# A fused two-layer kernel on one core: high products of the first expert tile ahead, block 0's matrices fetched by two queues, gate table loaded first

## What is computed

```python
w = weights[subjects]                                    # 8 matrices 64x64, one chosen per sample
y = einsum('bct,bcd->bdt', x, w)                         # "mix"
gate, up = split(y @ ternary(w_gate_up).T)               # 2048 each; weights quantized in groups of 64
h = silu(gate) * up
x = x + rms_norm(h) @ ternary(w_proj).T                  # layer 0
H = x @ W.T + scal * ((x @ A[idx].T) @ Bm[idx].T)        # one of 8 rank 16 adapters per sample
logits = (H @ router_w.T + router_b).reshape(T, 512, 8)  # 8 logits per token AND output column
c = weights of the top 2 of softmax(logits), renormalized, scattered over the 8 experts
    # c[t, e] sums over the 512 columns
x = x + sum_e c[t, e] * (H @ expert_w[e].T + expert_b[e])   # layer 1
```

## Time and profile before

| | |
|---|---|
| median of 3 runs | 2350.64 us (2349.07 to 2351.0) |
| the profiled execution | 2351.97 us |
| its span | 2350.2 us, 30421 instructions |
| granted TensorE clock, mean | 0.995 |
| VectorE busy | 1669.3 us, 71% |
| ScalarE busy | 1148.8 us, 49% |
| GpSimd busy | 8.9 us |
| moved by DMA | 184.61 MB, mean 79 GB/s |

### The profile page before, as it was taken

One profiled execution on the slowest core, in us unless ns is written; L12 is line 12 of the kernel. 1 busy time (PEld: TensorE's weight loads), 2 busy tenths in 40 slices (PEclk: granted clock), 3 DMA queues, 4 the chain that ended last, 5 costly groups with the idle time before them and its releaser, 6 DMA issues.

```text
span 2350.2 us, 30421 instructions
## 1 busy us (share of the span) xinstructions
PE 2301.7 (98%) x10280; PEld 1897.4 (81%) x10288; DVE 1669.3 (71%) x2497; ACT 1148.8 (49%) x1685; POOL 8.9 (0%) x16
## 2 busy tenths in 40 slices
PE   6999999999999999999999999998899999999999
PEld 5777888888888887888888888887688888888887
DVE  7985434334343435888888888999988888888883
ACT  6764333323332324788888888887322222222221
POOL 0000000000000000000000000000000000000000
PEclk9999999999999999999999999999999999999999
DMA  5314202111111115211111111215322222222220
GB/s 197 105 44 137 74 19 74 43 54 51 54 54 37 71 36 201 75 65 62 62 54 66 58 58 63 67 62 182 142 91 87 94 78 78 94 80 76 94 80 22
DMA packets 106589, 184.61 MB, mean 79 GB/s; under 512 B 12466, under 2 KB 45746, under 8 KB 105266
## 3 DMA queue, kind: packets, MB, share of 16 engines
q1 hardware_dynamic: 54946, 124.84, 15.2%
q10 hardware_dynamic: 51600, 59.25, 7.6%
HBM read 122.72 MB, written 61.34 MB: 78 GB/s over the span
## 4 chain that ended last, share of the span: by engine, by line
PE 90%; issue 5%; DVE 3%; ACT 1%; DMA 1%; ACTq 0%; SPq 0%; POOL 0%; POOLq 0%; DVEq 0%
PE slot L1445 17%; PE plane L1576 10%; PE plane L1578 10%; PE plane L1580 10%; PE ex L1618 10%; PE ex L1620 10%; PE ex L1622 10%; PE pj L1458 8%; PE slot L1498 3%; PE slot L1420 1%; PE slot L1487 1%; PE slot L1477 1%; PE slot L1430 0%; DMA eraw<-in_ewT 0%; DMA eb_sb<-in_eb 0%
## 5 line engine op out<-in xcount | busy, mean ns | idle before, releaser
L1618 PE MATMUL ex<-ew_hi,hb 128*128 128x512 f32 x1024 | 400.8, 391 | 16.6 <-DVE ew_lo L1332 11.3
L1445 PE MATMUL slot<-y_hi,wgu 128*128 128x512 f32 x1024 | 403.1, 394 | 2.3 <-DVE q_scale L1002 1.2
L1576 PE MATMUL plane<-rw_hi,hb 128*128 128x512 f32 x1024 | 399.5, 390 | 1.6 <-ACT plane L834 0.9
L1620 PE MATMUL ex<-ew_hi,hb 128*128 128x512 f32 x1024 | 400.4, 391 | 0.0
L1622 PE MATMUL ex<-ew_lo,hb 128*128 128x512 f32 x1024 | 400.3, 391 | 0.0
L1578 PE MATMUL plane<-rw_hi,hb 128*128 128x512 f32 x1024 | 399.2, 390 | 0.0
L1445 PE MATMUL slot<-y_lo,wgu 128*128 128x512 f32 x1024 | 399.1, 390 | 0.0
L1580 PE MATMUL plane<-rw_lo,hb 128*128 128x512 f32 x1024 | 399.1, 390 | 0.0
L942 ACT ACTIVATE ex<-eb_sb 128x512 f32<-128x512 f32 x248 | 149.3, 602 | 460.0 <-DVE acc L1371 395.8
L1304 DVE SCALAR_TENSOR_TENSOR lead_in<-code_in,wts 128x1024 bf16<-128x1024 bf16 x256 | 311.5, 1217 | 1.8 <-DVE code_in L1249 0.4
L1618 PEld LDWEIGHTS ex<-ew_hi,hb 128*128 128x128 f32 x1024 | 193.4, 189 | 58.5 <-issue 7.9
(11 more groups left out here) (128 smaller groups left out, 3148.3 us busy)
## 6 DMA issues: line engine op xcount, KB each, us to landing
hb<-h_scratch SPq DMA_DIRECT2D x34, 512.0 KB, 3.3
h_scratch<-ht ACTq DMA_DIRECT2D x64, 256.0 KB, 3.0
code_scratch<-half_code SPq DMA_DIRECT2D x64, 256.0 KB, 2.0
half_in<-code_scratch SPq DMA_DIRECT2D x32, 512.0 KB, 3.3
hb<-h_scratch ACTq DMA_DIRECT2D x30, 512.0 KB, 3.6
q_raw<-in_w_ffn SPq DMA_DIRECT2D x21, 512.0 KB, 3.4
x_scratch<-x_res ACTq DMA_DIRECT2D x8, 1024.0 KB, 4.4
rraw<-in_rwT SPq DMA_DIRECT2D x8, 1024.0 KB, 11.0
```

The source lines that it names most:

```text
L1445: last = mm(slot[s % 2][:, g, :], wgu[:, c, r * P:(r + 1) * P], y[:, c, :], start=(c == 0 and v == 0), stop=(c == DC - 1 and v == 1))
L1576: mm(plane[b][:, :, :], hb[:, u, c, 0, :], rw_hi[:, w, c, o], start=False, stop=False, skip_group_check=True)
L1618: mm(ex[e][:, :], hb[:, u, c, 0, :], ew_hi[:, e, c, :], start=(first and c == 0), stop=False, skip_group_check=True)
L1620: mm(ex[e][:, :], hb[:, u, c, 1, :], ew_hi[:, e, c, :], start=False, stop=False, skip_group_check=True)
```

## The change

1. Block 0's eight gathers are shared: SyncE fetches samples 0 to 3 (`mixw_in`), GpSimd samples 4 to 7 (`mixw0_in`), ahead of its constants. TensorE waits for both.
2. SyncE's next loads change order: x_res and three gathers for block 1, then raw tiles 3 and 4, then the other five gathers.
3. ScalarE runs a Silu of one column as its first activation, and the first `square` waits for it.
4. Expert weights lie in DRAM as one run of 8 KB for each expert and partition (before: four of 2 KB), loaded without the spill of tile NT-2 between them.
5. `eb_sb` lies in the memory of `bias_sb` and is loaded once the last plane is seeded, ahead of that spill; `xin` is loaded after the last half's tournament, behind the spill and the loads of tile 2's lead and codes.
6. TensorE does the 64 products with `ew_hi` of tile 0 for all experts, then the 32 with `ew_lo`.
7. ScalarE makes the six splits 2 to 7 ahead of the last two `stand`. VectorE does the last half without its join, splits 3 to 7, the eight expert steps of tile 0, the two joins, the eight bias steps, and decode and totals of tile 2 by themselves; then tiles 1 and on as before.
8. ScalarE's first pair of tiles is written out: the seeds after tile 0 come ahead of the weighing of tile 2, and the store of tile 0 waits for the bias steps.

```diff
+        eb_sb = sb("eb_sb", [P, E, D], F32, p4)
+        p4.close()
         bias_sb = sb("bias_sb", [P, 2, E, HO], F32, p2)
...
-            gather_mix(0, mixw, mixw_in)
+            gather_mix(0, mixw, mixw_in, range(SPB // 2))
...
+            sp.dma_start(x_res[:, :, :], one(XB, 1)).then_inc(xmix1_in, 16)
+            gather_mix(1, mixw1, mixw1_in, range(3))
             load_raw(3)
             load_raw(4)
-            sp.dma_start(x_res[:, :, :], one(XB, 1)).then_inc(xmix1_in, 16)
-            gather_mix(1, mixw1, mixw1_in)
+            gather_mix(1, mixw1, mixw1_in, range(3, SPB))
...
-                    sp.dma_start(eraw[:, e, :, :], EWT[e]).then_inc(eraw_in[e], 16)
-                if b == 0:
-                    spill(NT - 2, 0, 2 * NT - 3, 2 * NT - 2, 2 * NT - 2)
+                    sp.dma_start(eraw[:, e, :, :].rearrange("p c o -> p (c o)"), ewT[e]).then_inc(eraw_in[e], 16)
             load_h(1, 1)
-            sp.wait_ge(joined, 2 * NT)
-            sp.dma_start(xin[:, 0, :], X1T[0]).then_inc(x1_in[0], 16)
+            sp.wait_ge(seeded, NT * PT)
             sp.dma_start(eb_sb[:, :, :], eb).then_inc(eb_in, 16)
-            sp.dma_start(xin[:, 1, :], X1T[1]).then_inc(x1_in[1], 16)
+            spill(NT - 2, 0, 2 * NT - 3, 2 * NT - 2, 2 * NT - 2)
             load_lead(2, 0)
             sp.wait_ge(decoded, 2)
             load_halves(2)
+            sp.wait_ge(lead_ready, 2 * NT)
+            sp.dma_start(xin[:, 0, :], X1T[0]).then_inc(x1_in[0], 16)
+            sp.dma_start(xin[:, 1, :], X1T[1]).then_inc(x1_in[1], 16)
             spill(NT - 1, 1, 2 * NT - 1, 2 * NT, 2 * NT)
...
         def _(pool):
+            pool.wait_ge(dconst, 1)
+            pool.wait_ge(subject_in, 16)
+            for q in range(SPB // 2, SPB):
+                v = pool.value_load(subject_i[0:1, q:q + 1], min_val=0, max_val=E - 1)
+                r = (q % 2) * C
+                pool.dma_start(mixw[r:r + C, q // 2, r:r + C], cond_w[bass.ds(v * C, C), :]).then_inc(mixw0_in, 16)
+
...
+            act.wait_ge(dconst, 3)
+            nc.scalar.activation(sq[:, 0:1], ones_col[:, :], ACT.Silu).then_inc(table_in, 1)
             quant_in(0)
...
-            split_expert(2)
+            for e in range(2, E):
+                split_expert(e)
             stand(NT - 1, 0)
-            split_expert(3)
-            split_expert(4)
             stand(NT - 1, 1)
-            for e in range(5, E):
-                split_expert(e)
...
             def store(n, u):
+                if isinstance(n, int) and n == 0:
+                    act.wait_ge(bias_step, E)
...
-                    weigh(m * 2 + (u + 2), u, m + 1)
+                    if not (isinstance(m, int) and u == 0):
+                        weigh(m * 2 + (u + 2), u, m + 1)
                     for e in range(E):
                         seed_expert(m * 2 + u, e)
+                    if isinstance(m, int) and u == 0:
+                        weigh(2, 0, 1)
...
             for e in range(3):
                 split_expert(e)
-            half(NT - 1, 1, 1, NT // 2 - 1)
-            split_expert(3)
-            split_expert(4)
-            join(NT - 1, 1)
-            for e in range(5, E):
+            half(NT - 1, 1, 1, NT // 2 - 1, joins=False)
+            for e in range(3, E):
                 split_expert(e)
...
+            def bias(e):
+
+                if e:
+                    dve.wait_ge(bias_step, e)
+                nc.vector.scalar_tensor_tensor((res if e == E - 1 else acc)[:, 0, :], eb_sb[:, e, :], c_ring[:, 0, e:e + 1],
+                                               acc[:, 0, :], ALU.mult, ALU.add).then_inc(bias_step, 1)
...
+            for e in range(E):
+                expert(0, e, 0, 0)
+            for s in range(2):
+                join(NT - 1, s)
             dve.wait_ge(eb_in, 16)
+            dve.wait_ge(exp_step, E)
             for e in range(E):
-                bias(0, e, 0, 1)
-            for n in range(4):
+                bias(e)
+            decode(2, 2)
+            for e in range(E):
+                total(2, e, 2)
+            for n in range(1, 4):
                 tile(n, n, n // 2)
...
-            experts(0, 0, first=True)
+            def first_experts():
+
+                pe.wait_ge(hb_in[0], NT // 2 * 16 + 16)
+                for e in range(E):
+                    if e >= 4:
+                        pe.wait_ge(evac, NT * PT - 3 + e - 4)
+                    pe.wait_ge(ehi, e + 1)
+                    for c in range(DC):
+                        for v in range(2):
+                            mm(ex[e][:, :], hb[:, 0, c, v, :], ew_hi[:, e, c, :], start=(c == 0 and v == 0), stop=False)
+                for e in range(E):
+                    pe.wait_ge(elo, e + 1)
+                    for c in range(DC):
+                        last = mm(ex[e][:, :], hb[:, 0, c, 0, :], ew_lo[:, e, c, :], start=False, stop=(c == DC - 1))
+                    last.then_inc(ex_filled, 1)
+
+            first_experts()
             experts(0, 1)
...
-        "ewT": g["L1_ffn_expert_w"].transpose(2, 0, 1).reshape(D, E * D),
+        "ewT": g["L1_ffn_expert_w"].reshape(E, D, DC, P).transpose(0, 3, 2, 1).reshape(E, P, DC * D),
```

More of the change, by code:

```diff
@@ L304, in build @@
         mixw_in = sem("mixw_in")
+        mixw0_in = sem("mixw0_in")
         xres_in = sem("xres_in")
@@ L412, in _, with gather_mix @@
         def _(sp):
-            def gather_mix(i, w, done):
-                for q in range(SPB):
+            def gather_mix(i, w, done, samples=range(SPB)):
+                for q in samples:
                     v = sp.value_load(subject_i[0:1, bass.ds(i * SPB + q, 1)], min_val=0, max_val=E - 1)
@@ L558, in _ @@
             load_halves(2)
+            sp.wait_ge(lead_ready, 2 * NT)
+            sp.dma_start(xin[:, 0, :], X1T[0]).then_inc(x1_in[0], 16)
+            sp.dma_start(xin[:, 1, :], X1T[1]).then_inc(x1_in[1], 16)
             spill(NT - 1, 1, 2 * NT - 1, 2 * NT, 2 * NT)
             def ahead(n, u, wait):
-                if isinstance(n, int) and n == 0:
-                    sp.wait_ge(bias_step, 1)
-                else:
-                    sp.wait_ge(exp_step, wait)
+                sp.wait_ge(exp_step, wait)
                 sp.dma_start(xin[:, u, :], one(X1T, n + 2)).then_inc(x1_in[u], 16)
@@ L686, in square @@
             def square(i, j, h):
-                if not (first_block(i) and j == 0):
+                if first_block(i) and j == 0:
+                    act.wait_ge(table_in, 1)
+                else:
                     act.wait_ge(ss_ready, i * HC + j)
@@ L1366, in expert @@
                     dve.wait_ge(summed, n * E + E)
-                    base = xin
                 dve.wait_ge(ex_filled, n * E + (e + 1))
@@ L1370, in expert @@
                     dve.wait_ge(out_done[u], trip * 16)
-                nc.vector.scalar_tensor_tensor((res if e == E - 1 else acc)[:, u, :], ex[e][:, :], c_ring[:, k, e:e + 1],
-                                               base[:, u, :], ALU.mult, ALU.add).then_inc(exp_step, 1)
+                nc.vector.scalar_tensor_tensor((res if e == E - 1 and not first else acc)[:, u, :], ex[e][:, :],
+                                               c_ring[:, k, e:e + 1], (xin if e == 0 else acc)[:, u, :],
+                                               ALU.mult, ALU.add).then_inc(exp_step, 1)
             def tile(n, k, pair):
```

43 lines of the change are left out of this document (15 added, 28 removed).

## The result

The median is **2340.11 us** (2339.09 to 2341.39, 6 runs) against 2350.82 for the kernel before in the same session (2349.07 to 2352.15, 6 runs): ratio 0.9955, 95% interval 0.9945 to 0.9965. The forecast was 2340.1. The profiled execution took 2339.39 us, its span is 2337.7, the granted clock 0.997.

The account below looks back on a forecast made before the run. TensorE was taken as the bound, busy 2301.7 of 2350.2 us. Gains of 2.7, 1.0 and 6.8 sum to 10.5; from the profiled 2351.97 that gives 2341.5, and 1.3 lower for the median, 2340.1; 8-in-10 range 2338.6 to 2345.6.

Parts of the forecast that it names:

- Gathers, -2.7: Start of block 0: sharing the eight gathers between SyncE and GpSimd lets the mix start at 11.3, saving 2.7 us.
- a margin of 2.4: Start of block 0: gathers landed by 8.9, while the mix needs them at 11.3.
- one of the signs of being wrong: Start of block 0: a wait of the mix for a transfer beyond 11.3 would show the prediction wrong.
- The rival of late gathers: Start of block 0: GpSimd's gathers land late, giving 2345.3 us, or 2342.7 in a middle case; chance 0.20.
- Table, -1.0: Before the first gate product: the early one-column Silu removes the later table load for which VectorE waited, saving 1.0 us.
- SyncE's order, 0: Start: SyncE's reordered loads delay nothing, raw tile 3 arriving with 2.4 us to spare; 0 us.
- Transition, the chain: First expert tiles: VectorE's work in its new order, from first split at 1629.32 to tile 1's first expert step at 1683.2.
- Transition, TensorE: First expert tiles: tile 2's e=1 begins at 1689.8 against 1696.58, saving 6.8 us.
- 2 to 6 us: First expert tiles: a new TensorE idle of this length stands before tile 2.
- lower clock beyond e=1: Transition rival: the lower clock outlasts the start of tile 2's e=1, costing 1.7 us; whole short-transition rival's chance 0.12.
- The sum: Whole kernel: gathers 2.7, table 1.0 and transition 6.8 add to a gain of 10.5 us.

Follow-up runs that it names:

- the experiment: All eight gathers of block 0 on SyncE again, with SyncE's loads in their old order, against the changed kernel: 2345.21 us, ratio 0.9973.
- the repeated pair: The changed kernel and the kernel before, each run once more unchanged: 2340.05 and 2350.29 us, one run each.

## Why the prediction was right, point by point

- **Gathers, -2.7: measured -2.4** (13.98 to 11.56; 2.3 by the experiment). SyncE's fourth goes out at 7.07 (computed 6.8), GpSimd's at 7.19. The step that was mis-sized is the landing: I took 2.1 us from the issue, so 8.9 on either queue, and a margin of 2.4. It took 4.4 us on SyncE's queue and 4.1 on GpSimd's, and the mix waited 0.18 us for SyncE's, until 11.56. That is one of the signs of being wrong that the prediction named. The 2.1 us were those of the eighth gather of the kernel before, issued when little else was in flight. The windows show it, first of the kernel before at that gather, then of the changed kernel at the fourth (us, busy of PE, PEld, DVE, ACT, POOL, granted clock, DMA share, GB/s):

```profile
11.90:14.00 2.10, 0.02 (x1) 0.05 (x1) 2.00 (x3) 0.36 (x1) 0.00 (x0) 1.00 0.26 55
```

```profile
7.00:11.50 4.50, 1.04 (x2) 0.13 (x2) 4.27 (x7) 2.11 (x3) 1.23 (x5) 1.00 1.05 361
```

At 361 GB/s all 16 DMA engines are busy, with raw tiles 1 and 2 and with x_res, which the change itself puts right behind the fourth gather. In the kernel before the fourth gather was in some 3.6 us after its issue. How much of the difference is x_res, no run here tells. In the kernel with the bias steps first the issues run 1.0 us later and the landing only 0.35 later, so the landing hardly follows the issue there. An error of 2.6 us in the landing cost 0.2, because TensorE's second mean keeps it until 11.38 in any case; that part of the hit is luck. The margin was all gone: in other executions of the same start the mix waits up to 0.79 (at 11.91, again with the bias steps first). The rival of late gathers named the wrong queue: both land late, and GpSimd's ahead of SyncE's. The Trainium skill ("DMA: Bandwidth & Descriptors", section "Issuing engines are not separate DMA queues") would have had the issue time "usually small"; here halving it was worth the 2.3 us. Its rule in "SBUF — State Buffer", section "SBUF: two separate sides", that GpSimd's DMAs starve beside a two-port operation of VectorE, does not show in these rows: the pitch of the issues stays 1.15 us, and GpSimd's gathers land no later than SyncE's beside them.
- **Table, -1.0: measured -0.97**, the whole of VectorE's idle (1.06 by the interval from TensorE's first gate and up product). Together with the mix's own length (5.52 for 5.70) the start gives 2.42 + 0.18 + 0.97 = 3.6 of the 3.66 seen at the first gate product. It passes on undiminished: `bias_sb` is loaded 3.77 earlier.
- **SyncE's order, 0**: raw tiles 3 and 4 go at 11.99 (computed 12.4), and no engine waits for them.
- **Transition, the chain.** Computed 53.9 from the first split (1629.32 to 1683.2), measured 53.48. By parts, computed and measured: three splits 6.6, 6.61; half 8.7, 8.86; five splits 11.1, 11.01; expert steps 6.3, 6.17; joins 1.4, 1.20; bias steps 6.3, 6.17; decode 3.4, 3.43; totals 10.1, 10.03. The totals do stand at 1.25 each without a partner. Tile 1's first expert step comes at 1676.93, not near 1679.5 as foreseen: 2.1 of that is the clock in the third column and no work of the change. xin was issued at 1639.04 and is not waited for, nor is the third expert's weight.
- **Transition, TensorE.** From the router's last product to tile 2's e=1 I computed 62.4 (1689.8 - 1627.38); it is 62.15, against 69.20 before: -7.05. The wait before tile 2, "2 to 6 us", is 4.80. That mark hides 0.4: tile 2's e=1 still begins at the lower clock until 1684.2, so the stretch to the end gains only 6.6 (722.82 - 716.20). The rival's "lower clock beyond e=1" came true at a quarter of its price. **-6.8 predicted, -6.6 measured** in this pair of executions, -5.7 in the repeated pair and -6.4 by the means.
- **The sum** had 10.5; the rows of the first pair give 10.3, the means over all executions 9.9 and the medians 10.7. That the forecast met the median of 2340.11 to the tenth is luck: a stretch of lower clock moves one execution by two, and the same interval differs by up to 0.9 between two executions of one kernel. What held is the mechanism of each term and its size to about half a microsecond.
- **What was not foreseen** is the idle of 3.6 us in the high products, 1.91 of it for the eighth expert's weights, whose load ends at 1637.5. The prediction had the weights in by 1641 in the old time, which is 1635.1 here, so 2.4 late; the bias table and other loads are issued from 1622.77 on, beside them. It cost nothing, since the low parts end later in any case.

## What to carry to other kernels

When the bound engine waits at a transition, write the feeding engine's work there as a chain with its prices, and ask of each link whether the next consumer needs it now: here eight totals and a decode for the tile after next stood in front of tile 1's first step, and moving them behind it won another 6.7 us (2340.11 to 2333.38). A reordering that is worth nothing alone may be worth something on top of another (here the high products: 0 alone, 2.1 us beside VectorE's new order), so test them alone and together. The time of a transfer from issue to landing holds only for the traffic in which it was read: 2.0 us for a gather at 55 GB/s were 4.4 at 361. And where single stretches of lower clock move a whole run by 2 us, compare kernels by intervals between marks, over more than one execution, before a median is believed.

## What the runs showed of the hardware that was not expected

- TensorE's granted clock falls in stretches whose length differs between executions of one kernel. The same work between two marks takes 178.6 us in seven of the fourteen traces and 180.7 to 180.9 in the other seven, nothing between; the clock falls there at a wait of 4.10 us that all fourteen have.
- At the start likewise. Of the five executions of the new start in which the mix begins by 11.69, none has the products at 20 us at the lower clock, and the first gate product comes at 24.17 to 25.16; of the four in which it begins between 11.82 and 12.23, three have (26.53 to 27.11; one of these is the kernel with the table load). So a late landing of the gathers may cost more than its wait of 0.2 us in some runs; four cases don't prove it, and the kernels with all gathers on one queue have the lower clock at the same place too (mix at 13.83 and 15.69), while the kernel before (13.98) does not.
- A DMA issued by GpSimd with a register for its address takes 0.52 to 0.70 us of the engine, one every 1.15 us; on SyncE it is one every 1.25 to 1.27. From the start of the issue to the landing these 16 KB gathers took 2.0 us with the DMA engines at a share of 0.26 (SyncE's eighth, kernel before) and, with all of them busy, 4.4 (SyncE's fourth, changed kernel), 4.1 (GpSimd's fourth, same kernel) and 3.9 (GpSimd's eighth, all on GpSimd). The difference goes with the traffic and not with the queue.
